# The gathered rows of a graph network with expert layers: where the expert tiles are turned

## What is computed

```python
x = x + gnn(layernorm(x), src, dst, W_in, b_in, W_out, b_out)
x = x + ffn(layernorm(x))

def ffn(x):                                   # E = 8 experts, D = 256, H = 512, top 2
    xn = layernorm(x) * gamma + beta
    logits = xn @ Wr + br
    top_vals, top_idx = top_k(logits, 2)
    w_full = one_hot(top_idx) * softmax(top_vals)
    for e in range(8):
        h = gelu(xn @ W1[e] + b1[e])
        y = y + (h @ W2[e] + b2[e]) * w_full[..., e, None]
    return y
```

## Time and profile before

| | us |
|---|---|
| median of 3 runs | 1216.51 |
| lowest and highest | 1213.09, 1216.91 |
| the profiled execution's own time | 1212.99 |
| its span | 1211.2 |
| first `hidden` of the expert layer, from the span's start | 1009.8 |
| TensorE busy over the span | 1150.2 |
| VectorE, ScalarE, GpSimd busy | 702.9, 418.2, 227.8 |

### The profile page before, as it was taken

One profiled execution on the slowest core, in us unless ns is written; L12 is line 12 of the kernel. 1 busy time (PEld: TensorE's weight loads), 2 busy tenths in 40 slices (PEclk: granted clock), 3 DMA queues, 4 the chain that ended last, 5 costly groups with the idle time before them and its releaser, 6 DMA issues.

```text
span 1211.2 us, 26287 instructions
## 1 busy us (share of the span) xinstructions
PE 1150.2 (95%) x7856; PEld 816.0 (67%) x7856; DVE 702.9 (58%) x1425; ACT 418.2 (35%) x806; POOL 227.8 (19%) x278
## 2 busy tenths in 40 slices
PE   5798999999999999999999999999999998999993
PEld 3686766766566666666666666666666666889993
DVE  7898999994444433443155424443254677776566
ACT  1566655663100000000022101211022236777682
POOL 2000000000011121111100000000022237567752
PEclk8998999999999999999999999999999999999998
DMA  6111011013334424443334313331224333223476
GB/s 159 55 43 39 27 31 30 25 34 102 86 92 93 90 57 110 95 102 64 69 107 130 99 43 97 107 102 52 37 90 128 111 113 91 88 80 94 124 212 190
DMA packets 77196, 105.98 MB, mean 87 GB/s; under 512 B 13559, under 2 KB 62510, under 8 KB 76988
## 3 DMA queue, kind: packets, MB, share of 16 engines
q1 hardware_dynamic: 63997, 75.26, 21.0%
q0 software_dynamic: 11376, 25.55, 9.4%
q10 hardware_dynamic: 1740, 4.11, 1.3%
HBM read 77.00 MB, written 37.49 MB: 95 GB/s over the span
## 4 chain that ended last, share of the span: by engine, by line
PE 78%; DVE 10%; DMA 4%; issue 3%; ACT 2%; DVEq 2%; POOL 1%; ACTq 0%; SPq 0%; POOLq 0%
PE ps L2000 45%; PE ps L2054 8%; PE ps L1978 7%; PE ps L1946 5%; PE ps L2168 4%; PE ps L2182 4%; DVE v_b L1239 4%; PE ps L1914 1%; DMA h_ring<-h_dram 1%; PE ps L1925 1%; DVE adj L1146 1%; DMA adj<-xs_dram,v_a 1%; PE ps L2082 1%; ACT v_b L1084 1%; POOL y_dram L855 0%
## 5 line engine op out<-in xcount | busy, mean ns | idle before, releaser
L2000 PE MATMUL ps<-v_a,adj 125*125 125x512 f16 x1375 | 297.3, 380 | 0.0
L2000 PE MATMUL ps<-v_b,adj 125*125 125x512 f16 x1250 | 270.2, 380 | 1.7 <-DVE v_b L1264 1.7
L2000 PEld LDWEIGHTS ps<-v_a,adj 125*125 (+1 forms) x1375 | 188.2, 137 | 108.3
L2000 PEld LDWEIGHTS ps<-v_b,adj 125*125 x1250 | 171.1, 137 | 100.5 <-issue 2.1
L959 ACT ACTIVATE t_hi<-ps,cinv 125x256 f32<-125x256 f32 x125 | 59.1, 473 | 454.9 <-PE ps L2000 396.6
L1246 DVE SCALAR_TENSOR_TENSOR t_hi<-ps,cinv,t_hi 125x256 f32<-125x256 f32 x125 | 60.3, 483 | 235.7 <-ACT t_hi L959 235.7
L1239 DVE TENSOR_TENSOR v_b<-v_b 125x2560 f16<-125x2560 f16 x125 | 180.3, 1488 | 6.1 <-PE ps L1946 5.5
L2054 PE MATMUL ps<-v_b,adj 125*125 125x512 f16 x625 | 139.8, 381 | 0.2 <-issue 0.2
L934 ACT ACTIVATE adj<-ps 125x625 f32 (+1 forms) x125 | 112.1, 906 | 65.7 <-PE ps L1946 64.8
L1978 PE MATMUL ps<-v_a,adj 125*125 125x512 f16 x500 | 122.8, 379 | 0.0
L2182 PE MATMUL ps<-adj,v_b 128*128 x672 | 110.0, 275 | 10.2 <-issue 8.5
(11 more groups left out here) (279 smaller groups left out, 992.2 us busy)
## 6 DMA issues: line engine op xcount, KB each, us to landing
h_ring<-h_dram SPq DMA_DIRECT2D x125, 125.0 KB
v_a<-L_ffn_W SPq DMA_DIRECT2D x32, 256.0 KB, 3.5
v_b<-L_ffn_W SPq DMA_DIRECT2D x32, 256.0 KB, 3.5
adj<-w_dram SPq DMA_DIRECT2D x16, 512.0 KB, 5.3
adj<-y_dram SPq DMA_DIRECT2D x8, 560.0 KB
w_dram<-w_hi SPq DMA_DIRECT2D x32, 128.0 KB, 1.9
hx_dram<-h_dram POOLq DMA_DIRECT2D x25, 125.0 KB, 2.4
hx_dram<-x POOLq DMA_DIRECT2D x25, 125.0 KB, 3.2
```

The source lines that it names most:

```text
L2000: last = te.matmul(ps[0:NP, u, :], of_tile(adj[0:NP, 0:ADJ], i, u, a * NP, NP), source[:, a, :], start=(a == 0), stop=(a == T - 1))
```

## The change

SyncE issues one transposing DMA for each tile, from `x_g[j % 8]` straight into `xT16[j % 4]`; TensorE's transposes, the PSUM banks that they used, ScalarE's copies and the semaphores between them are gone. A tile is turned when its gather has landed and `hidden(j - 4)` is done with the buffer. GpSimd's gathers and TensorE's `hidden(j)` wait for the transfer instead. The first one waits for `v_read`, which TensorE raises when tile 24 of the last step has read the four blocks under `xT16`. The other DMAs of SyncE are placed between the turned tiles: the last six `rows_out` behind tiles 3 and 9 to 13, the loads of lots 0, 1 and 2 behind tiles 46, 47 and 48, the first store behind tile 53.

```diff
+        LOADS_AT = 46
-        TURN_AT = (T - 10, T - 5)
@@ SyncE
-            for w in range(T - 6, T):
-                rows_out(w, w % WIN)
+            def turned(j):
+                sp.wait_ge(g_in[j % FU], 16 * (j // FU + 1))
+                need(sp, S["ffn_h"], j - XR + 1)
+                sp.dma_start_transpose(xT16[j % XR], x_g[j % FU]).then_inc(x_turned[j % XR], 16)
...
-            sp.wait_ge(S["tok_ps"], 2)
-            sp.wait_ge(S["idx_ok"], 2)
-            landed(0)
-            for n in range(3):
-                for k in range(TOP):
-                    load(n, k)
-            store(0)
+            sp.wait_ge(S["v_read"], 1)
+            for j in range(FT):
+                turned(j)
+                if j == XR - 1:
+                    rows_out(T - 6, (T - 6) % WIN)
+                if 9 <= j < 9 + WIN:
+                    rows_out(T - WIN + j - 9, j - 9)
+                if j == LOADS_AT:
+                    landed(0)
+                if LOADS_AT <= j < LOADS_AT + 3:
+                    for k in range(TOP):
+                        load(j - LOADS_AT, k)
+                if j == FT - 3:
+                    store(0)
             store(1)
@@ GpSimd, gather(j)
-                    pool.wait_ge(S["xg_T"], j - FU + 1)
+                    pool.wait_ge(x_turned[(j - FU) % XR], 16 * ((j - FU) // XR + 1))
@@ ScalarE
-            def transposed(j):
-                act.wait_ge(S["xg_T"], j + 1)
-                need(act, S["ffn_h"], j - XR + 1)
-                a.activation(xT16[j % XR], ps[:, turn_bank(j), :].bitcast(F16)[:, 0:2 * D].rearrange("k (b s) -> k b s", b=2 * DK),
-                             ACT.Copy).then_inc(S["xgT_ok"], 1)
@@ TensorE, the last step
-                        if m == T - 1 and a in TURN_AT:
-                            transposed(TURN_AT.index(a))
+                        if m == T - 1 and a == XR - 1:
+                            last.then_inc(S["v_read"], 1)
@@ TensorE, the tiles
-            def transposed(j):
-                u = j % FU
-                pe.wait_ge(g_in[u], 16 * (j // FU + 1))
...
-                for b in range(2 * DK):
-                    last = te.transpose(ps[:, turn_bank(j), :].bitcast(F16)[:, b * 128:(b + 1) * 128], x_g[u][:, b * 128:(b + 1) * 128], ident16)
-                last.then_inc(S["xg_T"], 1)
...
-                    if j < LAG:
-                        pe.wait_ge(S["xgT_ok"], j + 1)
+                    pe.wait_ge(x_turned[j % XR], 16 * (j // XR + 1))
...
-                if b == 0 and not alone:
-                    pe.wait_ge(S["xgT_ok"], j + LAG + 1)
@@ ffn_tiles
-            if b == 0 and 0 < j < count - 2:
-                transposed(j + 2)
```

More of the change, by code:

```diff
@@ L402, in gnn_ffn @@
         g_in = [sem(f"g_in{r}") for r in range(FU)]
+        x_turned = [sem(f"turned{r}") for r in range(XR)]
         y_out = [sem(f"y_out{r}") for r in range(FR)]
@@ L428, in turned_in @@
             return [w for w in range(T) if turn_slot(w) == m]
-        def turn_bank(j):
-            return 2 if j == 0 else (j - 1) % 2
         def rows_place(w):
@@ L1871, in tables_ready @@
                 pass
-            ffn_tiles(dve, FT, FA, LAG, (experts, parts), 1, transposed, hidden, result, between, tables_ready)
+            ffn_tiles(dve, FT, FA, LAG, (experts, parts), 1, hidden, result, between, tables_ready)
             for n in range(3, len(LOTS)):
```

20 lines of the change are left out of this document (3 added, 17 removed).

## The result

The changed kernel takes 1220.83 us in the median of 5 runs (1219.88 to 1221.43), beside 1214.13 us for the kernel before in the same session. The ratio is 1.0053 (95% interval 1.0039 to 1.0067): slower by half a per cent, where 1211 us and a gain were forecast. The profiled execution has a span of 1219.1 us, against 1211.2.

What follows compares the result with a forecast made beforehand. TensorE was taken as the bound from 1074 to 1182 us. The terms -8.5 - 1.5 + 0.5 + 4.0 gave -5.5 us, so 1211.0 us against the median of 1216.5, with a range of 1204 to 1228.

Steps and rivals of the forecast that it cites:

- Part 1: Transposes leave TensorE: 8.5 us gained in loops 17 to 53, 1.5 us before loop 17, GpSimd costing nothing.
- Part 3: The start: the first turned tile lands late for hidden(0), charged 0.5 us (0 to 1.9).
- Part 4: Lots 0 to 2 jam with turned rows: TensorE stands at hidden(49), charged 4 us (0 to 9).
- Part 2: SyncE's turning: 1.0 us of SyncE and 0.42 us of the DMA engines per tile, keeping pace with 2.65 us loops.
- B: Rival: SyncE too slow per turning instruction; at 4.1 us each, about 1267 us; chance 0.10.
- C: Rival: a tile's four blocks turned one after another, 7.6 us per tile, about 1449 us; chance 0.06.
- theory J-load: Follow-up theory: around loops 42 to 50 the 16 DMA engines have more to move than fits, whoever issues it.
- Rival A: Each 256-byte piece costs a 1 KB packet: 1.6 us per turned tile, jam 9.3 us, 1216 us; chance 0.22 with its kin.

Runs made afterwards that it cites:

- e5: Kernel before with one TensorE transpose per tile in place of four and no DMA instead (output partly wrong): 1210.72 us, ratio 0.9976.
- e19: SyncE turning only tiles 3 to 43, plus four small GpSimd fills ahead of scatters 14 to 43, against the kernel before: 1211.56 us, ratio 0.9978.
- e9: SyncE turns only tiles 3 to 43, TensorE the others, lot reads behind tile 43's turning; against the kernel before: 1210.62 us, ratio 0.9979.
- e12: Kernel before with one transpose per tile in place of four, and lots 0 to 2 reading one node tile of five: 1209.29 us, ratio 0.9975.
- e13: Changed kernel with lots 0 to 2 reading one node tile of five, against the kernel before: 1208.73 us, ratio 0.9969.
- e10: SyncE turns tiles 0 to 43, TensorE the rest, lot reads behind tile 43's turning; against the kernel before: 1211.21 us, ratio 0.9977.
- e7: Changed kernel with the six lot reads issued one behind each of turned tiles 44 to 49, against the kernel before: 1220.88 us, ratio 1.0052.
- e3: Changed kernel with reads of lots 0 to 2 on ScalarE's queue at loops 42 to 44, against the kernel before: ratio 1.0109.
- e18: Changed kernel with reads of lots 0 to 2 on ScalarE's queue, repeated on the other 1246 us chip, against the kernel before: ratio 1.0109.
- e2: Changed kernel with tiles 0 and 1 turned ahead of the last step's last rows_out, against the kernel before: 1253.68 us, ratio 1.0063.
- e4: Changed kernel with a second transposing DMA of half a tile from tile 4 on, into an unread buffer; against the kernel before: 1262.0 us, ratio 1.0137.
- e6: Kernel before with lots 0 to 2 held back until hidden(42), (43) and (44): 1246.27 us, ratio 1.0006.
- e11: SyncE turning only tiles 3 to 43, reads of lots 1 and 2 waiting for hidden(42), (43), (45), (46); against the kernel before: 1211.05 us, ratio 0.9986.

## Why the prediction was wrong, step by step

By the spans the forecast was -5.5 us and the profile has +7.9, which is 13.4 apart. Of these, 2.75 lie before loop 17 (Parts 1 and 3: -1.0 forecast, +1.75 measured), 1.05 in loops 17 to 43, and 9.3 in loops 43 to 55, where 4.0 for the jam less 2.5 for transposes were forecast and 10.8 measured. The term that was mis-sized is Part 4's; Part 1 has an error of its own, which the change hides and e5 shows.

**Part 1, right in size and wrong in reach.** The loop is 2.65 us, and from loop 17 to 43 the trace has 4.95 us of the 6.0 forecast. The step that failed is "all on the path, since TensorE is the bound there". It is the bound up to loop 43 and not behind. In loops 43 to 49 the DMA engines have 13.3 us of lots to bring, and TensorE finds its rows when these let them through: e5 gains 2.9 us by the medians where 6.8 were expected. Before, 0.4 us at 1156.13 was the tip of this: TensorE then arrived just ahead of the gather. In e5 it arrives there 3.2 us earlier, the gather lands only 0.8 us earlier, and the stand grows by 2.5 us, with the lower clock behind it. The stand was read as a small cost and was a bound with next to no slack.

GpSimd has a part in it. The prediction took it to cost nothing, because it isn't what TensorE waits for. VectorE's y of tile 37 and GpSimd's scatter of it, before and after:

```profile
1144.53 0.48 DVE L1868 SCALAR_TENSOR_TENSOR adj<-ps,v_a,adj 128x256 f32<-128x256 f32 x1 [0.29 <-issue]
```

```profile
1145.37 1.03 POOL L855 DMA_INDIRECT y_dram<-adj,v_a  x1 [0.30 <-DVE adj L1868]
```

```profile
1142.14 0.48 DVE L1860 SCALAR_TENSOR_TENSOR adj<-ps,v_a,adj 128x256 f32<-128x256 f32 x1 [0.43 <-issue]
```

```profile
1144.68 1.00 POOL L863 DMA_INDIRECT y_dram<-adj,v_a  x1 [0.30 <-issue]
```

Before, GpSimd follows at once. After, it is 2 us behind: it comes out of the routing loops late in both kernels, and where TensorE's loop is 2.65 us it doesn't catch up, while at 2.88 it does, with 2.57 from scatter to scatter until it has. So y was 2.4 us earlier and the gather behind that scatter only 0.7. That its lag costs time of its own isn't shown: in e19 the stand at loop 45 is 3.09 us, and the ratio is that of e9 (0.9978 and 0.9979). With small lots (e12) there is no such stand, so the lag alone doesn't make it.

Before loop 17 the 1.5 us taken were nothing: the stands there end with VectorE's y, and the last of them grew (1.66 us at loop 17, 1.09 before).

**Part 2, right about the pace.** SyncE's instruction takes 1.19 us for 1.0, and there is no stand for turned rows from loop 5 to 46. The engines need 0.72 to 0.77 us per tile for 0.42, which costs nothing here and enters Part 4. The forecast leaned on "Advanced Engine Details and Errata", section "X-Bar Transpose (TRN2)", of the Trainium skill; by these rows the turning costs the engines 1.7 to 1.8 times what the gather's or scatter's equal bytes cost before, so it isn't as fast as a regular transfer, though far from 1309 ns a block ("VectorE: DVE Perf Modes", "The three transpose paths"): four blocks take SyncE 1.2 us in all. B and C are out.

**Part 3.** 0.5 us (at most 1.9) was charged, and the first `hidden` of the profile stands 2.79 us where it stood 0.96. Whether that reaches the end is another matter: among kernels that start like the one before, on the faster kind of chip, the tile-0 scatter lies between 1026.8 and 1029.3 us, and in e9 and e19 the first `hidden` stood 2.12 and 2.86 us for weights. So the 1.75 us at loop 17 in one profile aren't shown to be a cost.

**Part 4, the step that failed.** The place was right to a loop and the size was not: 4 us at `hidden(49)` (0 to 9) against 9.6 at 47 to 49, and 2.65 more for the loop behind them at the lower clock, which the sum had no term for. Its working took the transfers too cheap. With 0.72 us per turned tile and 1.0 per tile for gathers and scatters, as measured ahead of the jam, loops 43 to 49 hold 13.3 + 7 x 1.72 = 25.3 us of transfers in 18.6 us; before, it was 13.3 + 7 x 0.84 = 19.2 in 20.2. So 6.8 us are missing, not 4.5. In the jam itself each tile is dearer still. The queues of 1146 to 1176, the lots' 13.3 us among the first:

```profile
q1 hardware_dynamic: 5061, 4.84, 67.4%
q0 software_dynamic: 800, 2.23, 35.0%
```

By their bytes these are 7.6 turned tiles beside the lots, and gathers and scatters of 8.5 tiles. That is 0.9 us for a turned tile and 1.2 for its gather and scatter, and 13.3 + 7 x 2.1 = 28.0 us in 18.6 leave 9.4 missing, close to the 9.6 measured. This is a balance and no proof, since transfers also last longer because the engines are full. Besides, a turned tile needs two transfers through the jam one after the other, a gather of 8.70 us and its turning of up to 14.30, where before it was one.

That the jam needs both the reads and the turning is shown: less reading (e13) or less turning (e9, e10) leaves no stand for turned rows, and another order on the same queue (e7) has 9.4 us against the change's 9.6. The reads on another queue don't remove it either (e3 7.2 us, e18 9.4, both on chips of 1246 us); that they make it longer there than SyncE's queue does (e2, 2.97) is what theory J-load leaves unexplained.

Rival A had the kind of mechanism (pieces dearer than taken, a jam of 9.3 us) and a time of 1216 (measured: 1220.83). That its jam fits is partly luck: it rests on 1.6 us a turned tile, about twice what was measured. What it lacked is the clock (2.65 us), VectorE's stand (1.9) and what the profile lost before loop 17 (2.75).

## What to carry to other kernels

Before counting an engine's saved time to the end, follow the path past the stretch where that engine is the bound, to the first place where another resource has no slack; a stand of 0.4 us in front of a full resource says that most of what is saved ahead of it may stop there (in e5, 2.5 of 3.2 us). Work moved from an engine to the DMA engines cost nothing that showed where these had room, and 0.84% where they had to read the lots, so split it by place: here SyncE turns tiles 3 to 43, TensorE the ones that meet the bulk reads, and the reads are spaced out, which makes 0.9964 of the kernel before (0.9979 without the spacing, a difference within the intervals).

## What the runs showed of the hardware

- A transposing DMA of 128x512 float16 values moves in 544 packets, of 241 bytes in the mean, and takes 0.72 to 0.77 us of the 16 engines where they have room, and 1.12 for half as much again (e4). Both kinds of instruction, 128 KB and 64 KB, hold SyncE for 1.2 us, so big ones are cheaper for it.
- Four chips fall into two kinds, 2.7% apart on the kernel before (1213 and 1246 us). On the slower kind TensorE stands between its own instructions (7.7 us in 80 in e6, none on the other), which is a part of the difference; no kernel whose rows SyncE turns gained there.
- TensorE's granted clock fell to its lower level for most of a loop behind stands of 2.12, 2.87 and 3.09 us (e9, e5, e19; 1.6 us lost in e5 and e9) and behind one of 7.34 us in the change (2.65 us lost); behind one of 2.14 us in e11 it stayed at 1.00.
- Ahead of each of GpSimd's indirect transfers 0.30 us pass; fills of 0.22 us in front of a scatter leave 0.16 of them, and the loop stays at 2.65 us (e19, at 1139 to 1143).
